# Layer 0's depthwise convolution in 64x64 tiles, with the work around it dealt out anew to ACT, POOL and DVE

## The chip, the cores and the metric

The kernel runs on one core of one Trainium2 chip. The metric is the device time in microseconds (us), the lower the better. The engines are TensorE (PE, with its weight loads shown as PEld), VectorE (DVE), ScalarE (ACT), GpSimd (POOL) and SyncE (SP, which here only issues DMAs). Each engine works through its own list of instructions in order; semaphores join the lists.

## The reference, cut to what matters

x is 8 samples of 256 positions by 256 features. Eight blocks follow each other, each added to x: cross-attention and a feed-forward part in each of four layers. The change lies in layer 0's feed-forward part, which for each sample is:

```
h = bit_linear(layernorm(x), w1)            # 256 -> 1024 features
h = silu(depthwise_conv1d(h, conv_w) + b)   # 3 taps over positions, each feature by itself
x = x + bit_linear(h, w2)                   # 1024 -> 256 features
bit_linear(x, w): per position, s = 127 / max|x|; round(x*s)/s, times w rounded to -1, 0, 1 (times mean|w|)
```

So each sample needs two maxima of absolute values per position: one over 256 features (in rows: positions on the partitions), one over 1024 hidden features (these lie on the partitions, 8 blocks of 128), and a rounding after each.

## The kernel before, in words

The stage is `ffn0`. Its lists are written out by hand: `ffn0_pe`, `ffn0_act`, `ffn0_dve` and `ffn0_pool`, each a loop over the samples i = 0 to 7; no planner orders them. In the round of sample i the stage works at once on the convolution of sample i, the first product of sample i+1 and the second product of sample i-1. Constants: B = 8 samples, S = 256 positions, T = 2 tiles of 128 positions, FC = 8 hidden blocks, PAIRS = 4 pairs of blocks.

One sample goes through these steps, with the lines of the profile. **Rows in:** DVE takes mean and variance (`ternary_stats`, L1290, L1293); POOL makes 1/sqrt (`ternary_rstd`, L198 and L201, a power); DVE normalizes (`quant_rows`, L1352), takes the largest absolute value (L1358), makes the scales in small instructions (L1363 to L1370), multiplies and rounds (L1372, L1374) and so releases `z_ready`. PE turns the rows (L1404, L1406), ACT copies them (L1393, L1394), PE makes the first product in pairs (L1417) and DVE multiplies each pair with the row of scales on its way out of PSUM (`first_kept`, L1381). **Convolution:** for each block PE adds up three products of a 128x128 diagonal matrix of taps with the block shifted by one position (`convolved`, L1642), all in f32. ACT adds the bias and takes the SiLU (`silus`, L1598) into one of two buffers `f_y`. **Second maximum:** DVE reduces four blocks at a time over the hidden blocks (`half_largest`, L1468), joins the halves (L1474), PE turns the result (`largest`, L1649), DVE reduces over the partitions and makes the scales (`scales`, L1479 to L1483), PE turns them back (`row2`, L1661), ACT copies them (L1588), POOL multiplies the SiLU's output with them in two halves (`scaled`, L1554), DVE rounds each half to bf16 (`rounded`, L1494), PE makes the second product (`second_made`, L1431), and DVE adds it to x (`second_added`, L1439).

Beside this PE makes the next attention's values and keys (`prepared`, L968, L1032) as filling, ACT keeps them (L800, L808, L809), and POOL clears a buffer in four pieces (`second_zeroed`, L1559). The last sample's second half is on DVE alone (`last_rounded`, L1504, L1505), its second product is made in the stage behind.

Rounding is an addition and a subtraction of 1.5 * 2^23: `v.tensor_scalar(f_aq[:, fs, :], f_y[i % 2][:, fs, :], ROUND, ROUND, ALU.add, ALU.subtract)`.

The rows of the weight w2 come by one DMA on SP's queue at 24.36 us and are there 7.4 us after; the first reader waits until 42 us or later.

## Time and profile before

| | |
|---|---|
| runs | 1155.62, 1160.81, 1163.85 us; median 1160.81 us |
| profiled execution | span 1158.0 us, the first to the last instruction; its own time is not given apart from the span |
| PE busy | 1103.8 us (95% of the span) |
| DVE busy | 772.5 us (67%) |
| POOL busy | 522.9 us (45%) |
| ACT busy | 430.0 us (37%) |
| mean granted TensorE clock | 0.989 of full speed |
| stage `ffn0` | about 138 to 285 us |

Busy time is an average over stages with different limits; the stage is read by itself in the rows below. Matmuls are pipelined, so a busy PE need not be at its peak.

### The profile page before, as it was taken

What the parts mean: (1) busy time and instruction counts of PE and PEld (TensorE: products, weight loads), DVE (VectorE), ACT (ScalarE), POOL (GpSimd) and SP (SyncE); (2) the same over time, 40 slices, a digit from 0 to 9 for tenths busy, and PEclk for the clock granted to TensorE, in tenths of its full rate; (3) what the DMA queues carried; (4) which work ended last, traced back from release to release, by engine and by line L of the source; (5) the groups of instructions that cost most, each with busy time, mean ns of one, the idle gap of its engine ahead of it and who ended that gap; (6) DMA issues with size and microseconds to landing.
All of it is one profiled execution on the core that took longest, in us unless ns stands there. A gap on an engine that the chain in (4) does not pass through costs nothing.

```text
span 1158.0 us, 21241 instructions
## 1 busy us (share of the span) xinstructions
PE 1103.8 (95%) x7601; PEld 919.3 (79%) x7601; DVE 772.5 (67%) x1711; ACT 430.0 (37%) x890; POOL 522.9 (45%) x505
## 2 busy tenths in 40 slices
PE   9999999999899999999989999999999999999997
PEld 5788888886778856898877999999998687875564
DVE  5899889997887645989962222222222899977784
ACT  2555533234555412121111222222222456654466
POOL 5655224356877121768866111100254757531343
PEclk9999999999999999999988999999999999999999
DMA  6999700000100020000135422311120200000001
GB/s 223 393 397 387 286 1 1 13 12 10 79 1 1 1 103 1 1 2 24 38 137 197 176 109 109 110 36 36 55 88 30 78 10 10 1 1 1 1 28 46
DMA packets 44182, 93.61 MB, mean 81 GB/s; under 512 B 3885, under 2 KB 17998, under 8 KB 41414
## 3 DMA queue, kind: packets, MB, share of 16 engines
q1 hardware_dynamic: 35702, 62.24, 14.9%
q0 software_dynamic: 7104, 29.14, 6.9%
q10 hardware_dynamic: 1296, 1.18, 0.3%
q8 instruction: 49, 0.80, 0.3%
q14 instruction: 31, 0.25, 0.1%
HBM read 39.02 MB, written 51.51 MB: 78 GB/s over the span
## 4 chain that ended last, share of the span: by engine, by line
PE 61%; DVE 21%; POOL 6%; issue 5%; ACT 4%; DMA 2%; POOLq 1%; PEldq 0%; another core or an unknown queue 0%; SPq 0%; DVEq 0%; PEld 0%; ACTq 0%
PE PS L2416 10%; PE PS L2426 10%; PE PS L1109 6%; PE PS L1925 4%; PE PS L2281 3%; PE PS L1122 3%; PE PS L1087 2%; PE PS L1077 2%; DVE scr L1468 2%; PE PS L2270 2%; PE PS L1642 2%; DVE scr L1494 2%; PE PS L1804 2%; POOL big L695 1%; PE PS L1035 1%
## 5 line engine op out<-in xcount | busy, mean ns | idle before, releaser
L2450 ACT ACTIVATE scr<-PS,W 128x128 f32<-128x128 f32 x148 | 53.6, 367 | 191.1 <-PE PS L2416 190.0
L2416 PEld LDWEIGHTS PS<-scr 128*128 128x128 f32 x992 | 116.4, 192 | 5.2 <-issue 2.0
L2416 PE MATMUL PS<-scr 128*128 128x128 f32 x992 | 118.6, 276 | 1.6 <-issue 1.6
L2426 PE MATMUL PS<-scr 128*128 128x256 f32 x496 | 112.2, 379 | 0.0
L2481 DVE TENSOR_SCALAR scr<-PS,W 128x128 f32<-128x128 f32 x148 | 51.2, 350 | 85.2 <-PE PS L2416 85.2
L727 POOL TENSOR_TENSOR scr<-scr,small 128x1232 f32<-128x1232 f32 x32 | 72.0, 2251 | 73.1 <-DVE small L478 72.8
L2426 PEld LDWEIGHTS PS<-scr 128*128 128x128 f32 x496 | 91.8, 190 | 11.2
L2487 DVE TENSOR_TENSOR scr<-PS,W 128x256 f32<-128x256 f32 x37 | 15.7, 425 | 127.1 <-PE PS L2426 122.3
L868 ACT ACTIVATE big<-PS 128x512 f32<-128x512 f32 x144 | 73.1, 523 | 69.1 <-PE PS L1087 67.7
L2527 POOL DMA_DIRECT2D expert_out<-scr x28 | 15.3, 547 | 160.5 <-DVE scr L2487 156.5
L1109 PEld LDWEIGHTS PS<-scr,big 128*128 128x128 f32 x640 | 81.0, 191 | 8.1 <-issue 5.1
L1642 PE MATMUL PS<-big,W 128*128 128x256 f32 x384 | 85.6, 379 | 0.0
L1087 PE MATMUL PS<-W,scr 128*128 128x128 f32 x480 | 76.3, 279 | 9.5 <-ACT big L846 3.0
L1109 PE MATMUL PS<-scr,big 128*128 128x34 f32 (+1 forms) x640 | 83.5, 271 | 1.0 <-ACT big L868 0.9
L1642 PEld LDWEIGHTS PS<-big,W 128*128 128x128 f32 x384 | 71.5, 189 | 9.6
L1087 PEld LDWEIGHTS PS<-W,scr 128*128 128x128 f32 x480 | 56.6, 150 | 20.3 <-ACT big L846 4.6
L1554 POOL TENSOR_TENSOR scr<-scr 128x1024 f32<-128x1024 f32 x14 | 32.9, 2373 | 68.0 <-ACT scr L1588 68.0
L2281 PE MATMUL PS<-W,scr 128*128 128x128 f32 x512 | 61.1, 278 | 2.5 <-DVE scr L2036 2.4
L2281 PEld LDWEIGHTS PS<-W,scr 128*128 128x128 f32 x512 | 58.5, 192 | 3.7 <-DVE scr L2036 3.5
L1804 PE MATMUL PS<-identb 128*128 128x512 bf16 x232 | 59.8, 400 | 0.3 <-ACT big L868 0.3
L863 ACT ACTIVATE scr<-scr 128x1232 f32<-128x1232 f32 x48 | 58.7, 1223 | 3.0 <-POOL scr L727 2.6
L1598 ACT ACTIVATE scr<-PS,W 128x256 f32<-128x256 f32 x64 | 26.9, 472 | 81.4 <-PE PS L1642 81.4
(418 smaller groups left out, 2496.4 us busy)
## 6 DMA issues: line engine op xcount, KB each, us to landing
expert_in<-zeros SPq DMA_DIRECT2D x1, 19712.0 KB, 60.5
expert_out<-zeros SPq DMA_DIRECT2D x1, 19712.0 KB, 113.2
scr<-ew_in POOLq DMA_DIRECT2D x12, 1024.0 KB, 6.6
scr<-expert_in SPq DMA_DIRECT2D x38, 128.0 KB
big<-ew_in POOLq DMA_DIRECT2D x4, 1024.0 KB, 8.9
expert_out<-scr POOLq DMA_DIRECT2D x28, 128.0 KB, 2.0
W<-pack SPq DMA_DIRECT2D x1, 2458.0 KB, 8.7
W<-pack SPq DMA_DIRECT2D x1, 2152.0 KB, 9.0
```

Of the source, the lines that this page charges most:

```text
L727: g.tensor_tensor(sc3, sc3, a_mx[u % 3].unsqueeze(2).broadcast_to([P, H, S2]), ALU.subtract).then_inc(s["sub_ready"], 1)
L863: a.activation(a_sc[lay][u % 3], a_sc[lay][u % 3], ACT.Exp, scale=scale).then_inc(s["p_ready"], 1)
L868: a.activation(a_PT[lay][u % 2][:, 4 * g:4 * g + n, :], bank(ring_bank(lay, "p", u, g), n * P).rearrange("p (c n) -> p c n", c=n), ACT.Cop ...
L1087: ins = pe.transpose(bank(b, P, k * P), a_sc[lay][u % 3][:, at:at + P], ident)
L1109: ins = pe.matmul(bank(6 + u % 2, n * (DH + 1), FIRST[c] * (DH + 1)), a_PT[lay][u % 2][:, c, :], a_VB[lay][:, c, 0:n, u // T, :], start=(c ...
L1642: ins = pe.matmul(bank(2 + p % 2, S, (f % 2) * S), f_taps[:, f, j, :], f_G[:, f, j:j + S], start=(j == 0), stop=(j == 2))
L1804: pe.matmul(bank(b, size, at), identb[:, :], identb[:, :].unsqueeze(1).broadcast_to([P, size // P, P]), start=True, stop=True)
L2281: ins = pe.matmul(bank(4, P, c * P), vp[:, t, c * P:(c + 1) * P], ident, start=(t == 0), stop=(t == B - 1))
L2416: ins = pe.matmul(bank(1 + f % 4, G), e_w1[slot][:, k, f * P:(f + 1) * P], e_xT[:, k, :], start=(k == 0), stop=(k == C - 1))
L2426: ins = pe.matmul(bank(5 + t, D), e_h[:, f, t * P:(t + 1) * P], e_w2[slot][:, f, :], start=(f == 0), stop=(f == FC - 1))
L2450: a.activation(e_h[:, f, :], bank(1 + f % 4, G), ACT.Relu, bias=moe_bias(e, f)).then_inc(s["h_act"], 1)
L2481: v.tensor_scalar(e_h[:, f, :], bank(1 + f % 4, G), moe_bias(e, f), 0.0, ALU.add, ALU.max).then_inc(s["h_dve"], 1)
```

## The change

**Convolution (PE).** A tap matrix is diagonal, so only its two 64x64 blocks on the diagonal hold anything. Each 128x128 product becomes two of 64x64; for a pair of blocks the four row and column quarters of the array are used: row half r, column half c. That takes 12 products for a pair in place of 6. The hidden features lie in another order afterwards, so w2's rows are loaded in that order by four DMAs of half the partitions each instead of one (SP's queue, ahead of the last part of the constants), and ACT makes the bias in that order by four small copies behind the attention before. Each pair now uses two PSUM banks.

**ACT** takes the normalized rows from DVE (`rows`) and makes |y| in two halves of 4x256 (`absolutes`). **DVE** takes the maximum of |y| by elementwise maxima, 512 wide twice, 512 and 256. **POOL** makes a shift beside the 1/sqrt and takes over both halves of the rounding, behind clearing and 1/sqrt. **Order:** `scales(i)` comes in round i, and no longer at the head of round i+1; DVE's `quantized(i+1)` therefore comes right behind the last `hidden` of the round before; the second product of sample i-2 is made in round i in place of that of i-1, and that of sample 6 after the last `largest`. Buffers for the factors of the second product become three. The stage `tail` reuses semaphores of this stage.

```diff
+        f_top = cut(4 * S).rearrange("p (n f s) -> p n f s", n=2, f=2)
         f_amax = cut(S)
+        f_abs = [t.rearrange("p (f s) -> p f s", f=PAIRS) for t in (cut(PAIRS * S), big[:, 3 * C * S * 2:3 * C * S * 2 + PAIRS * S])]
...
+        f_deq2 = [csmall(T) for _ in range(3)]
+        f_bias = csmall(FC)
...
+        HALF = P // 2
+        IN_FFN = 16 * (2 + 4)
+
+        def hidden_halves(t):
+
+            return t.rearrange("p (u r n) -> p u r n", u=PAIRS, r=2)
+
+        def hidden_rows_sp(sp):
+
+            new, old = hidden_halves(f_w2), hidden_halves(w2T_in)
+            for c in range(2):
+                for r in range(2):
+                    sp.dma_start(new[c * HALF:(c + 1) * HALF, :, r, :],
+                                 old[r * HALF:(r + 1) * HALF, :, c, :]).then_inc(in_ffn, 16)
+
+        def hidden_biases(a):
+
+            a.wait_ge(in_ffn, IN_FFN)
+            new, old = hidden_halves(f_bias), hidden_halves(w["conv_b"])
+            for c in range(2):
+                for r in range(2):
+                    a.activation(new[c * HALF:(c + 1) * HALF, :, r, :], old[r * HALF:(r + 1) * HALF, :, c, :],
+                                 ACT.Copy).then_inc(ffn0["w_ready"], 1)
...
+        ROW2 = [4] * (B - 1) + [0]
+        KV_BANK = [4] * (B - 1) + [6]
+        AMAX_BANK = 0
+
+        def conv_bank(i, p, r):
+
+            return (2, 3)[r] if p % 2 == 0 else (0, 1)[r] if (i, p) == (B - 1, PAIRS - 1) else (5, 6)[r]
...
-                quant_rows(v, ch, i)
+                v.wait_ge(s["rows_ready"], i)
...
-                v.wait_ge(s["silu_ready"], PAIRS * i + 2 * n + 2)
-                ch.inc(v.tensor_reduce(f_top[:, n, :], f_y[i % 2][:, n * PAIRS:(n + 1) * PAIRS, :].rearrange("p f s -> p s f"),
-                                       AX.X, ALU.max, apply_absolute_value=True))
+                v.wait_ge(s["abs_ready"], 2 * i + n + 1)
+                v.tensor_tensor(f_top[:, n, :, :], f_abs[n][:, 0:2, :], f_abs[n][:, 2:4, :], ALU.max).then_inc(s["abs_used"], 1)
 
             def largest(i):
 
-                ch.sync()
-                v.tensor_tensor(f_amax, f_top[:, 0, :], f_top[:, 1, :], ALU.max).then_inc(s["amax_ready"], 1)
+                v.wait_ge(s["abs_used"], 2 * i + 2)
+                ch.link(v.tensor_tensor(f_top[:, 0, :, :], f_top[:, 0, :, :], f_top[:, 1, :, :], ALU.max))
+                v.tensor_tensor(f_amax, f_top[:, 0, 0, :], f_top[:, 0, 1, :], ALU.max).then_inc(s["amax_ready"], 1)
...
-            def rounded(i):
-
-                if i:
-                    v.wait_ge(s["o_psum"], i)
-                for n in range(2):
-                    fs = slice(n * PAIRS, (n + 1) * PAIRS)
-                    v.wait_ge(s["scaled_ready"], 2 * i + n + 1)
-                    v.tensor_scalar(f_aq[:, fs, :], f_y[i % 2][:, fs, :], ROUND, ROUND, ALU.add,
-                                    ALU.subtract).then_inc(s["aq_ready"], 1)
...
             for i in range(B):
-                if i:
-                    scales(i - 1)
                 if i + 1 < B:
                     quantized(i + 1)
+                if i == B - 1:
+                    sample_stats(v, ch, 1, 1)
+                half_largest(i, 0)
                 if i + 2 < B:
                     ternary_stats(v, ch, i + 2)
+                elif i == B - 2:
+                    sample_stats(v, ch, 1, 0)
                 else:
-                    sample_stats(v, ch, 1, i + 2 - B)
-                half_largest(i, 0)
-                if i == B - 1:
                     sample_rows(v, 1, 1)
-                if i:
-                    rounded(i - 1)
-                if i == B - 1:
                     sample_stats(v, ch, 1, 2)
                     query_vars(v, ch, 0)
-                half_largest(i, 1)
-                largest(i)
                 if i + 1 < B:
                     hidden(i + 1, (0, 1))
-                if i:
-                    second_added(v, i - 1)
+                half_largest(i, 1)
                 if i + 1 < B:
-                    hidden(i + 1, (2, 3))
+                    hidden(i + 1, (2,))
+                largest(i)
+                scales(i)
+                if i >= 2:
+                    second_added(v, i - 2)
+                if i + 1 < B:
+                    hidden(i + 1, (3,))
                 if i >= 5:
                     key_vars(v, ch, i - 5)
                 if i == B - 2:
                     sample_rows(v, 1, 0)
-            scales(B - 1)
+            second_added(v, B - 2)
...
-            def scaled(i):
+            def scaled(i, n):
                 g.wait_ge(s["row2_ready"], i + 1)
-                for n in range(2):
-                    fs = slice(n * PAIRS, (n + 1) * PAIRS)
-                    y = f_y[i % 2][:, fs, :]
-                    g.tensor_tensor(y, y, f_row2.unsqueeze(1).broadcast_to([P, PAIRS, S]),
-                                    ALU.mult).then_inc(s["scaled_ready"], 1)
+                y = f_y[i % 2][:, n * PAIRS:(n + 1) * PAIRS, :]
+                g.tensor_tensor(y, y, f_row2.unsqueeze(1).broadcast_to([P, PAIRS, S]),
+                                ALU.mult).then_inc(s["scaled1_ready" if n else "scaled0_ready"], 1)
+
+            def rounded(i, n):
+                if i:
+                    g.wait_ge(s["o_psum"], i)
+                fs = slice(n * PAIRS, (n + 1) * PAIRS)
+                g.wait_ge(s["scaled1_ready" if n else "scaled0_ready"], i + 1)
+                g.tensor_scalar(f_aq[:, fs, :], f_y[i % 2][:, fs, :], ROUND, ROUND, ALU.add,
+                                ALU.subtract).then_inc(s["aq1_ready" if n else "aq0_ready"], 1)
...
             for i in range(B):
                 if i:
-                    scaled(i - 1)
-                if i + 2 < B:
-                    ternary_rstd(g, i + 2)
+                    scaled(i - 1, 1)
+                    scaled(i - 1, 0)
                 if i == 1:
                     g.wait_ge(at_["o_full"], NT)
                 if 1 <= i <= 4:
                     second_zeroed(i - 1)
+                if i + 2 < B:
+                    ternary_rstd(g, i + 2)
+                if i:
+                    rounded(i - 1, 0)
+                    rounded(i - 1, 1)
...
+            def rows(i):
+
+                a.wait_ge(rstd_ready, i + 1)
+                a.wait_ge(z_ready, T * i)
+                for t in range(T):
+                    ins = a.activation(f_z[:, t, :], X[:, T * i + t, :], ACT.Identity,
+                                       bias=f_shift[i % 2][:, t:t + 1], scale=f_rstd[i % 2][:, t:t + 1])
+                ins.then_inc(s["rows_ready"], 1)
+
+            def absolutes(i, n):
+
+                a.wait_ge(s["silu_ready"], PAIRS * i + 2 * n + 2)
+                if i:
+                    a.wait_ge(s["abs_used"], 2 * i + n - 1)
+                a.activation(f_abs[n], f_y[i % 2][:, n * PAIRS:(n + 1) * PAIRS, :], ACT.Abs).then_inc(s["abs_ready"], 1)
...
+            rows(1)
             for i in range(B):
                 silus(i, 0)
-                silus(i, 1)
                 if i:
                     row2(i - 1)
+                silus(i, 1)
+                absolutes(i, 0)
                 if i == B - 1:
                     extra_kept(a, 1, "z", 0)
                 silus(i, 2)
+                if i + 1 < B:
+                    normed(i + 1)
+                silus(i, 3)
+                absolutes(i, 1)
+                if i + 2 < B:
+                    rows(i + 2)
                 if i == B - 1:
                     extra_kept(a, 1, "q", 0)
-                silus(i, 3)
-                if i + 1 < B:
-                    normed(i + 1)
                 if i < 4:
-                    values_kept(a, 1, i, 5)
+                    values_kept(a, 1, i, KV_BANK[i])
                 else:
-                    rows_kept(a, i - 4, 5)
+                    rows_kept(a, i - 4, KV_BANK[i])
...
-                for f in (2 * p, 2 * p + 1):
-                    for j in range(3):
-                        ins = pe.matmul(bank(2 + p % 2, S, (f % 2) * S), f_taps[:, f, j, :], f_G[:, f, j:j + S],
-                                        start=(j == 0), stop=(j == 2))
+                for j in range(3):
+                    for r in range(2):
+                        rows = slice(r * HALF, (r + 1) * HALF)
+                        for c in range(2):
+                            f = 2 * p + c
+                            ins = pe.matmul(PS[c * HALF:(c + 1) * HALF, conv_bank(i, p, r), 0:S],
+                                            f_taps[rows, f, j, rows], f_G[rows, f, j:j + S],
+                                            start=(j == 0), stop=(j == 2))
...
+            pe.wait_ge(at_["y_done"], PTILE(0, NT - 2) + 1)
             for i in range(B):
                 convolved(i, 0)
                 convolved(i, 1)
                 if i:
                     row2(i - 1)
-                if i == B - 1:
-                    extra_made(pe, 1, "z", 0)
                 convolved(i, 2)
                 if i == B - 1:
                     pe.wait_ge(s["row2_ready"], i)
+                    extra_made(pe, 1, "z", 0)
+                convolved(i, 3)
+                if i == B - 1:
                     extra_made(pe, 1, "q", 0)
-                convolved(i, 3)
                 if i + 1 < B:
                     normed(i + 1)
+                if i >= 2:
+                    if i == 2:
+                        pe.wait_ge(s["w_ready"], C + 4 + 1)
+                    second_made(pe, i - 2)
+                for p in range(PAIRS - 1):
+                    if i + 1 < B:
+                        hidden(i + 1, p)
                 prepared(i)
                 if i + 1 < B:
-                    hidden(i + 1, 0)
-                    hidden(i + 1, 1)
-                if i:
-                    if i == 1:
-                        pe.wait_ge(s["w_ready"], 3)
-                    second_made(pe, i - 1)
+                    hidden(i + 1, PAIRS - 1)
                 if i == B - 1:
-                    clocked(pe, 6, 8)
+                    pe.wait_ge(s["silu_ready"], PAIRS * i + PAIRS - 1)
+                    clocked(pe, 2, 8)
                 largest(i)
-                if i + 1 < B:
-                    hidden(i + 1, 2)
-                    hidden(i + 1, 3)
+            second_made(pe, B - 2)
```

## Rows read from the trace of the kernel before

**Rows 1.** Stretches of the stage: us; each engine busy (instructions); clock, DMA, GB/s.

```profile
155.69:255.44 99.75, 99.56 (x591) 84.60 (x590) 96.23 (x188) 31.48 (x75) 45.68 (x30) 1.00 0.03 8
255.44:284.70 29.26, 27.80 (x166) 21.97 (x165) 23.45 (x50) 11.97 (x25) 16.45 (x9) 1.00 0.00 1
```
**Rows 2.** Order of time, 172 to 189 us: start, us, engine, line, operation, tiles, count.

```profile
172.19 5.35 PE L1642 MATMUL PS<-big,W 128*128 128x256 f32 x24
...
173.62 0.41 DVE L1479 TENSOR_REDUCE small<-PS 128x2 f32<-128x256 f32 x1
...
174.94 0.73 DVE L1352 TENSOR_SCALAR big<-X,W 128x256 f32<-128x256 f32 x2
...
175.71 0.69 DVE L1358 TENSOR_REDUCE small<-big 128x2 f32<-128x512 f32 x1
176.43 0.17 DVE L1363 TENSOR_SCALAR small<-small 128x2 f32<-128x2 f32 x1
...
178.09 0.43 DVE L1374 TENSOR_SCALAR W<-big 128x512 bf16<-128x512 f32 x1
...
178.77 4.68 POOL L1554 TENSOR_TENSOR scr<-scr 128x1024 f32<-128x1024 f32 x2 [9.40 <-ACT scr L1588]
...
181.24 3.35 DVE L1494 TENSOR_SCALAR scr<-scr 128x1024 bf16<-128x1024 f32 x2
...
182.78 0.27 PE L1404 MATMUL PS<-W 128*128 128x128 f32 x1
...
184.98 1.04 PE L1417 MATMUL PS<-big,W 128*128 128x256 bf16 x8
...
187.60 0.38 PE L1649 MATMUL PS<-W,scr 128*128 128x128 f32 x2
...
188.03 0.87 DVE L1439 SCALAR_TENSOR_TENSOR X<-PS,small,X 128x256 f32<-128x256 f32 x2
```
**Rows 3.** Groups by line, 110 to 290 us: shapes, count | busy us, mean ns | idle.

```profile
L1468 DVE TENSOR_REDUCE scr<-scr 128x256 f32<-128x1024 f32 x16 | 30.9, 1934 | 4.9 <-ACT scr L1598 4.9
L1598 ACT ACTIVATE scr<-PS,W 128x256 f32<-128x256 f32 x64 | 26.9, 472 | 81.4 <-PE PS L1642 81.4
L1381 DVE TENSOR_TENSOR big<-PS,W 128x512 f32<-128x512 f32 x32 | 20.6, 684 | 1.0 <-PE PS L1417 0.8
```
**Rows 4.** Order of time, from 126 us: the first sample's quantization.

```profile
126.37 2.25 POOL L727 TENSOR_TENSOR scr<-scr,small 128x1232 f32<-128x1232 f32 x1 [3.77 <-DVE small L478]
...
127.16 1.48 DVE L1363 TENSOR_SCALAR small<-small 128x2 f32<-128x2 f32 x1
```
**Rows 5.** Order of time, from 297.5 us: POOL and DVE in turn.

```profile
298.01 2.19 POOL L710 TENSOR_TENSOR X<-X,W 128x512 f32<-128x512 f32 x2
298.15 2.20 DVE L423 TENSOR_SCALAR big<-X,small 128x256 f32<-128x256 f32 x2 [0.67 <-POOL small L201]
```
**Rows 6.** Order of time, from 268 us: small powers on POOL.

```profile
270.89 0.69 POOL L201 TENSOR_TENSOR small<-small,neghalf 128x2 f32<-128x2 f32 x1
...
271.55 5.43 POOL L695 TENSOR_TENSOR big<-big,neghalf 128x32 f32<-128x32 f32 x1
...
275.69 0.17 DVE L1480 TENSOR_SCALAR small<-small 128x2 f32<-128x2 f32 x1
```
**Rows 7.** Order of time, 55 to 62 us: products in 32-row tiles.

```profile
58.38 0.81 PE L1077 MATMUL PS<-scr,big 32*128 32x154 f32 x16
...
59.12 1.09 PE L1109 MATMUL PS<-scr,big 128*128 128x34 f32 x8
```
**Rows 8.** ACT's groups by line over the whole span.

```profile
L863 ACT ACTIVATE scr<-scr 128x1232 f32<-128x1232 f32 x48 | 58.7, 1223 | 3.0 <-POOL scr L727 2.6 <-DVE scr L467 0.4
...
L876 ACT ACTIVATE scr<-X,small 128x256 f32<-128x256 f32 x16 | 8.7, 591 | 1.9 <-POOL small L209 1.9
```
**Rows 9.** POOL's writing without reading, 110 to 290 us.

```profile
L1559 POOL MEMSET scr<- 128x1224 f32 x2 | 2.2, 1120 | 0.0
```
**Rows 10.** Order of time, from 135 us: the table load ahead of the first SiLU.

```profile
139.97 1.28 ACT L1598 ACT_TABLE_LOAD   x1
```

91 lines of the change are left out of this document (49 added, 42 removed).

## The prediction

> **What bounds the kernel now.** I read the stretches first, since the change touches one stage. Between the convolutions of samples 1 and 7 there are six rounds in 99.75 us, 16.6 us each; PE is busy for 99.56 of them, but DVE for 96.23 too, ACT for 31 and POOL for 46 [rows 1]. So two engines are full at once, and relieving PE alone gives nothing. The order of time [rows 2] shows what fills them. PE: 24 of a round's 48 convolution instructions take 5.35 us with the last one's tail, so about 0.216 us each and 10.4 us a round; all else on PE is 6.2 us. DVE: two reductions of 1.93 us [rows 3], and the two roundings, 3.35 us together. That last number is the one to see: the first of them starts at 181.24, just behind the start of POOL's second multiplication (the two run from 178.77 for 4.68 us), and the pair takes 3.35 us where the instruction's own work is below 0.7 us each. DVE waited there for POOL.
>
> The same wait in its purest form: a DVE instruction on 2 elements, usually 0.17 us [rows 2], takes 1.48 us when it meets a POOL multiplication that ends at 128.62 [rows 4]. And where two DVE instructions meet two POOL ones, they alternate: each DVE one waits out one POOL one, and two of them take 2.20 us in place of the 0.73 us of two like them [rows 5, 2]. Reductions aren't held: L1468 begins beside POOL's first multiplication in most rounds and still takes 1.93 us on the mean [rows 3].
>
> **The change part by part**, T = 0 being the end of a round's `largest` on PE, everything for one round in steady state.
>
> *Convolution.* 96 instructions of 64x64 in place of 48. Rows of the trace with tiles: 16 instructions with 32 rows and 154 columns start at 58.38, and the next product can start at 59.12: 0.046 us each where 154/256 of 0.216 is 0.130 us, so 2.8 times as fast with the way in and out of the tiling, four side by side [rows 7]. I take four side by side: 96 x 0.216 / 4 = 5.2 us, plus 0.25 us for a change of tiling and back, twice (0.74 us less 4 x 0.130). Bounds: row halves alone side by side, 10.4 us; nothing side by side, 20.8 us. I stay with 5.2 because the row halves are shown and the column halves touch other outputs. No row has column tiles. The Trainium skill, TensorE: Matmul & The Clock Gate, Part 3, gives 2.38 times for three column tiles; by it 5.2 us would be an estimated 6.6 us, and my sum would rise by 1 us at most, since PE waits anyway. Saved on PE: 4.7 us a round.
>
> *DVE loses* the reductions (3.9), the roundings (3.4), L1352 (0.73) and gains 512-wide maxima (0.66 each by the pace of L1381's 0.68 [rows 3], three of them) and one of 256 (0.4): 2.4 us for the 0.4 of before. It falls from 16 to about 10.5 us. *ACT gains* two |y| of 1024: 1.05 us each (1.22 us for 1232 columns at 0.83 ns [rows 8]; bounds 0.9 to 1.2), and two normalizing tiles, 0.54 each [rows 8]; it stays under 9 us. *POOL gains* two roundings of 1024 and a longer 1/sqrt (1.5 us: 0.69 for the power [rows 6] and three small ones of about 0.27). POOL has no such rounding in the trace: the lower bound is a write alone, 1.12 us for 1224, so 0.94 for 1024 [rows 9]; the upper bound is its two-input product, 2.34 us [rows 2]. One input lies nearer to the write: 1.1 us. The Trainium skill, GPSIMD Engine Reference, section 3.1, has 1.03 cycles an element for short bodies; by it the estimate is 0.9 us and the sum 2.4 us less. POOL then works 4.7 + 2.2 + 1.5 + 1.1 = 9.5 us.
>
> By busy time nobody is above 11.5 us. But almost every DVE instruction that is left reads SBUF alone, and POOL is now at work for most of the round, so the held instructions decide. **The loop:**
> - to 3.7: PE makes two pairs (2.6), changes tiling (0.25), turns the scales (0.3), ACT copies them (0.4); POOL starts its two multiplications.
> - Meanwhile DVE: scales 1.3 (173.62 to 174.94) [rows 2], `second_added` 0.87, last `hidden` 0.64, the reduction L1358 0.70: at 3.8 it stands before L1363, just behind POOL.
> - L1363 waits until 6.1, L1364 for the second multiplication until 8.6. From there L1364 to L1374 take 1.8 us (176.6 to 178.4) [rows 2]: 10.4. Without waits it would be 5.9. PE, which needs this for its next turn, has been idle since 6.2.
> - PE's turn and ACT's two copies 1.7 (12.1), SiLU 0.84 (13.0; its last pair now stands behind these copies on ACT), |y| 1.05 (14.1).
> - POOL's 1/sqrt waits for DVE's statistics behind all this (12.0), so until 13.5, and then two roundings until 15.8. DVE's second half maximum waits for them: 16.5; `hidden` 0.64, two more maxima 1.05: 18.2; PE's turn: 18.5.
>
> So a round of 18.5 us instead of 16.6. Drawn through with the same durations, the first two of the six come to 17.0 and 17.6, mean about 17.8: 6 x 1.2 = +7.2. The first round (15.54 us) has no multiplication on POOL and comes to 13.1: -2.4. It starts later than it could: ACT now makes two tiles of rows (1.08) and four small bias copies ahead of the table load of 1.28 us [rows 10]. The last piece (29.26 us [rows 1]) gains in convolution, but the second product of sample 6 (1.9) and DVE's addition now lie between the last maximum and the last sample's rounding: +1.4. SP issues three DMAs more, about 1.4 us ahead of the last constants; the first reader comes over 10 us later, so nothing. The wait for `y_done` ahead of the first convolution asks for an addition two tiles back, nothing.
>
> Sum: 7.2 - 2.4 + 1.4 = +6.2; 1158.0 + 6.2 = 1164.2 for the profiled execution, which lies 2.8 below the median: **1167 us**.
>
> One rule speaks for still more waiting. The trace has small powers on POOL of 5.43 us, and beside one a two-number instruction of DVE takes its usual 0.17 us [rows 6], so I let only multiplications and roundings hold DVE. The Trainium skill, SBUF — State Buffer, "Who interferes with whom", says the shared ports are held for the whole instruction; by that rule the powers would add up to 1 us a round. The measurement decides.
>
> **Rivals.**
> - *Faster: the waits don't line up.* If DVE comes to L1363 some 2 us before POOL, or its row of seven instructions passes together once it has its turn, the round falls to what remains: 18.5 less 4.5 (quantization) and 1 (maxima) = 13.1 us by the same drawing without any hold, -3.5 x 6, and in all about -26: 1135 us. One wait only, not two, gives 1150. For it: DVE and POOL meet within 0.1 us in my drawing, so small shifts matter. Against it: moving the meeting by 1 us changes which instruction waits, not that two do, and the alternation in rows 5. Chance 0.30.
> - *Slower: POOL's rounding costs like its product.* 2.34 us in place of 1.1; both lie between the 1/sqrt and DVE's maximum, so 2.2 us a round, +14: 1181 us. It decides from about 1.6 us on, where the time passes the 1% mark. For it: POOL does two operations and a conversion. Chance 0.13.
> - *The tiles don't do what they say:* column halves one after the other. PE then has 10.4 + 6.2 + the changes; round 18.7 to 19 us, +13 on top of my sum: 1180 us; with nothing side by side 29 us a round, beyond 1240. Chance 0.10, the latter 0.02 of it.
> - PE idle for over 4 us in each round may cost granted clock, now 1.00 throughout the stage [rows 1]; PE has slack there, so I count at most 1 us a round, within the range.
>
> **How the numbers follow.** About 1%, 11.6 us, is what can be told from no change: faster is below 1149, slower above 1172. The forecast's own case has 0.44 and runs from 1159 to 1177; 0.36 of it is within 1% and 0.08 above. The faster rival puts 0.28 below and 0.02 within. The two slow rivals (0.23) give 0.20 above and 0.03 within; the remaining 0.03 is spread. So faster 0.29, same 0.42, slower 0.29. As both signs hold much, the range must take in the unhindered case and the dear rounding: 1134 to 1182, with 0.1 left out at either end.
>
> **What will show it.** Right: DVE's L1363 and L1364 successors lasting 1.5 to 2.4 us beside POOL's products in each round; a gap on PE of about 4 us ahead of the turn of the next sample's rows; 96 convolution instructions in about 5.5 us; rounds of 17 to 18.5 us; POOL's rounding at 1.0 to 1.3 us. Wrong: DVE's small instructions at 0.2 us there and rounds of 13 to 14 us, or a POOL rounding above 1.6 us, or convolution instructions at 0.1 us each and more.

## The result, and the profile after

The change made the kernel slower: 1193.95 us (median of 4 runs, 1189.18 to 1197.85) against 1159.93 us before (1155.62 to 1163.85), a ratio of 1.030 (95% interval 1.026 to 1.034). I had forecast 1167 us in a range of 1134 to 1182, so the time lies outside the range. The profiled execution spans 1189.3 us, the one before 1158.0: +31.3. One of the four executions of the kernel with two buffers below (1195.59 us) fell in a slower state that shows a lower granted clock, and its figures leave that one out.

All of it lies in this stage. The last second product (L1431 before, L1463 now) ends at 284.7 before and at 316.2 now, +31.5; what follows takes 873.3 and 873.1 us. The stretches answer to [rows 1]: from the second sample's convolution to the last sample's, and from there to the end of the last second product.

```profile
154.83:266.94 112.11, 83.48 (x861) 55.99 (x860) 91.44 (x166) 48.17 (x97) 80.80 (x48) 0.88 0.03 7
266.94:316.24 49.30, 30.08 (x229) 20.42 (x229) 29.18 (x51) 14.05 (x27) 31.39 (x15) 0.79 0.00 1
```

Six rounds went from 99.75 to 112.11 us and the last piece from 29.26 to 49.30. PE, nearly full before, is now busy for 83 of 112 us; DVE for 91. POOL went from 46 to 81, and the granted clock of TensorE from 1.00 to 0.88 and 0.79. No engine is full: each now waits for the others. The groups of 138 to 317 us show which instructions grew (shapes, count | busy us, mean ns | idle before, releaser):

```profile
L1591 POOL TENSOR_SCALAR scr<-scr 128x1024 bf16<-128x1024 f32 x14 | 51.5, 3698 | 14.9 <-PE PS L1463 14.9
L1711 PE MATMUL PS<-big,W 64*64 64x256 f32 x768 | 48.4, 398 | 5.9 <-ACT scr L1643 5.9
...
L1463 PE MATMUL PS<-big,scr 128*128 128x256 bf16 x128 | 21.6, 341 | 2.3 <-DVE X L1471 2.3
...
L1402 DVE TENSOR_SCALAR big<-big,small 128x256 f32<-128x256 f32 x14 | 16.7, 1232 | 0.0
...
L1436 PE MATMUL PS<-W 128*128 128x128 f32 x14 | 4.9, 366 | 17.9 <-DVE W L1404 17.8
```

The same group of the second product before, from 110 to 290 us:

```profile
L1431 PE MATMUL PS<-big,scr 128*128 128x256 bf16 x128 | 15.3, 273 | 0.0
```

The first row is the surprise: POOL's rounding of one half takes 3.70 us, 7.3 us for a sample. L1402 (the multiplication of the quantization, L1372 before) shows the hold that I had looked for, a DVE instruction that lasts until POOL's is through: it takes 0.61 us for two when nothing is in the way, and 1.23 us for one on the mean here. The last is what it costs PE: 17.8 us of waiting for the quantized rows of L1404. One round in order of time (start, us, engine, line, tiles, count [idle before, releaser]):

```profile
205.44 3.63 POOL L1591 TENSOR_SCALAR scr<-scr 128x1024 bf16<-128x1024 f32 x1
...
209.19 0.84 ACT L1643 ACTIVATE scr<-PS,small 128x256 f32<-128x256 f32 x2 [3.59 <-POOL scr L1591]
...
210.17 2.82 PE L1711 MATMUL PS<-big,W 64*64 64x256 f32 x48 [1.16 <-ACT scr L1643]
...
210.38 4.71 POOL L1583 TENSOR_TENSOR scr<-scr 128x1024 f32<-128x1024 f32 x2 [1.31 <-ACT scr L1630]
210.43 5.87 DVE L1402 TENSOR_SCALAR big<-big,small 128x256 f32<-128x256 f32 x2
...
216.40 0.43 DVE L1404 TENSOR_SCALAR W<-big 128x512 bf16<-128x512 f32 x1
...
216.89 0.33 PE L1436 MATMUL PS<-W 128*128 128x128 f32 x1 [3.89 <-DVE W L1404]
...
217.39 3.09 PE L1463 MATMUL PS<-big,scr 128*128 128x256 bf16 x16
...
220.57 3.63 POOL L1591 TENSOR_SCALAR scr<-scr 128x1024 bf16<-128x1024 f32 x1 [0.69 <-PE PS L1463]
```

It reads as a circle. The roundings end, ACT's first SiLU of the next sample has waited 3.59 us for them, the convolution waits for ACT, and the row of scales lets POOL multiply. DVE's two L1402 meet the two multiplications and take 5.87 us. PE idles 3.89 us, then runs the second product, which takes 3.09 us, part of it at the lower clock, against 1.91 before (L1431, 282.76 to 284.67); and the next rounding waits for that product, since it writes the buffer that it reads. The stretches during PE's wait and in the second product (the number after POOL's instructions is the clock):

```profile
212.00:216.00 4.00, 0.99 (x20) 0.47 (x12) 4.00 (x2) 0.85 (x3) 4.00 (x3) 1.00 0.00 0
218.50:220.50 2.00, 2.00 (x12) 1.38 (x11) 0.00 (x0) 1.97 (x4) 1.22 (x4) 0.50 0.19 50
```

PE is busy for 0.99 of 4 us, and then works at half clock, 1.2 GHz.

The last two samples lose most. POOL's queue carries the powers of attention 1 behind the roundings:

```profile
261.39 7.44 POOL L1591 TENSOR_SCALAR scr<-scr 128x1024 bf16<-128x1024 f32 x2 [6.62 <-PE PS L1463]
...
269.78 5.91 POOL L681 TENSOR_TENSOR small<-small,neghalf 77x16 f32<-77x16 f32 x2
...
272.94 5.06 DVE L423 TENSOR_SCALAR big<-X,small 128x256 f32<-128x256 f32 x2
...
275.51 4.70 POOL L1583 TENSOR_TENSOR scr<-scr 128x1024 f32<-128x1024 f32 x2
...
286.17 7.23 POOL L1591 TENSOR_SCALAR scr<-scr 128x1024 bf16<-128x1024 f32 x2 [5.97 <-PE PS L1463]
...
294.39 0.74 DVE L423 TENSOR_SCALAR big<-X,small 128x256 f32<-128x256 f32 x2 [13.63 <-POOL small L201]
...
298.69 0.69 PE L1719 MATMUL PS<-W,scr 128*128 128x128 f32 x2 [9.15 <-DVE scr L1515]
```

The multiplications of sample 6 start at 275.51, behind L681, though their row of scales was copied by 270.55; DVE's two L423 (0.74 us at 294.39) take 5.06 us at 272.94, as the first waits out a power, L681, and the second a multiplication, and PE waits 6.55 us for them; DVE then waits 13.63 us for a reciprocal root that stands behind the last pair of roundings, and the last maxima stand behind that on DVE, so PE waits 9.15 us for them.

### The profile page after: what moved, and what is told of

Read it like the earlier page. It is cut to its first block, busy times and chain, and to the rows that moved or that the text cites. A ratio compares the mean times of both kernels' runs of the same rounds, so it can differ in the third digit from the quotient of the medians.

```text
span 1189.3 us, 22100 instructions
## 1 busy us (share of the span) xinstructions
PE 1088.7 (92%) x7985; PEld 887.0 (75%) x7985; DVE 771.1 (65%) x1691; ACT 453.6 (38%) x924; POOL 573.1 (48%) x533
## 4 chain that ended last, share of the span: by engine, by line
PE 60%; DVE 18%; POOL 9%; issue 6%; ACT 4%; DMA 2%; POOLq 1%; PEldq 0%; DVEq 0%; SPq 0%; ACTq 0%; PEld 0%
PE PS L2484 10%; PE PS L2494 10%; PE PS L1109 6%; PE PS L1993 3%; PE PS L2349 3%; PE PS L1122 3%; PE PS L1087 2%; PE PS L1077 2%; PE PS L2338 2%; PE PS L1872 2%; POOL big L695 1%; PE PS L1035 1%; DMA expert_out<-scr 1%; DVE big L1402 1%; POOL scr L1591 1%
## 5 line engine op out<-in xcount | busy, mean ns | idle before, releaser
L1591 POOL TENSOR_SCALAR scr<-scr 128x1024 bf16<-128x1024 f32 x14 | 51.5, 3698 | 14.9 <-PE PS L1463 14.9
L695 POOL TENSOR_TENSOR big<-big,neghalf 128x32 f32<-128x32 f32 x8 | 45.0, 5620 | 24.0 <-DVE big L431 23.7
L1122 PE MATMUL PS<-W,big 128*128 128x256 f32 x192 | 53.6, 402 | 0.8 <-ACT big L889 0.7
L1711 PE MATMUL PS<-big,W 64*64 64x256 f32 x768 | 48.4, 398 | 5.9 <-ACT scr L1643 5.9
```

The lines of the kernel that those rows point to most:

```text
L695: g.tensor_tensor(a_qr[j % 2], a_qvar[j % 2], neghalf[:, 0:T * H], ALU.pow).then_inc(s["qr_ready"], 1)
L1122: ins = pe.matmul(bank(6 + u % 2, D, D), a_OT[lay][:, c, :], wo[:, c, :], start=(c == 0), stop=(c == C - 1))
L1591: g.tensor_scalar(f_aq[:, fs, :], f_y[i % 2][:, fs, :], ROUND, ROUND, ALU.add, ALU.subtract).then_inc(s["aq1_ready" if n else "aq0_ready"], 1)
```

## The experiments

Three properties of the changed kernel turned out to matter: who rounds, when POOL's multiplications start, and the convolution's tiles. The times, with the distances between the starts of successive pairs of multiplications read from each trace; and how long the six rounds and the last piece of the stage are, bounded as the two stretches above:

| kernel | us | ratio to before, 95% | rounds between multiplications, us | six rounds | last piece |
|---|---|---|---|---|---|
| before | 1157 to 1160 | | 16.5 x5, 17.3 | 99.8 | 29.3 |
| changed: tiles, rounding on POOL | 1193.95 | 1.030 (1.026 to 1.034) | 17.9 16.7 17.3 19.4 20.3 25.4 | 112.1 | 49.3 |
| changed, rounding on DVE | 1180.11 | 1.019 (1.015 to 1.023) | 18.4 19.5 20.3 20.6 19.6 20.5 | 118.9 | 36.2 |
| changed, late multiplications | 1171.14 | 1.011 (1.008 to 1.015) | 16.3 17.3 16.5 17.3 16.7 20.1 | 99.4 | 44.6 |
| changed, both | 1154.90 | 0.997 (0.995 to 0.999) | 15.1 16.1 15.4 15.9 15.5 12.8 | 92.1 | 36.3 |
| changed, whole tiles | 1179.46 | 1.019 (1.015 to 1.022) | 16.8 17.4 17.4 17.4 17.4 21.1 | 103.7 | 45.0 |
| whole tiles, rounding on DVE | 1174.74 | 1.015 (1.011 to 1.020) | 18.0 18.6 18.6 18.6 18.6 18.6 | 110.8 | 33.6 |
| whole tiles, both | 1176.26 | 1.015 (1.012 to 1.018) | 18.0 18.6 18.6 18.6 19.2 17.9 | 110.9 | 34.9 |

"Late multiplications" and "both" are explained below. The kernel before has medians of 1157.3 to 1159.9 us in the four sets of runs, and what follows the stage, the same code in all, takes 869.2 to 876.5 us in the profiled executions; so a difference of 2 or 3 us between two rows is not settled, and the last two columns say more about the stage than the totals.

**Rounding back on DVE.**

```diff
-                if i:
-                    rounded(i - 1, 0)        # POOL
-                    rounded(i - 1, 1)
...
                 if i + 1 < B:
                     hidden(i + 1, (0, 1))
+                if i:
+                    rounded(i - 1)           # DVE, both halves
                 half_largest(i, 1)
```

> The changed kernel with one part undone: both halves of the rounding are back on DVE (after the first two pairs of the next sample's hidden values), POOL keeps the two multiplications. Theory A (POOL's rounding is the loss): in the changed kernel the pair of roundings takes 7.23 to 7.5 us on POOL against the 2.2 us I summed, it lies between the second product of the sample before and the first silu of the next sample, and in the last two samples the powers of attention 1 stand behind it on POOL. Then this kernel loses all of it: rounds of 16 to 17 us, 1135 to 1165 us. Theory B (the loss is DVE held by POOL's multiplications, 4.7 us a round, which stay): 1180 to 1195 us. Theory C (the loss is TensorE's granted clock at its lower level in the stage, for another reason than idle time caused by the rounding): 1175 to 1195 us with a mean clock still near 0.966.

1180.11 us (1178.86 to 1182.29), clock 0.973. Theory A alone is refuted: 14 us came back, not 30 to 60. And the table shows where: the last piece is 13.1 us shorter, while the six rounds are 6.8 us longer, as DVE now has the roundings and PE waits 25.0 us for L1404 in place of 17.8. So in the six rounds the dear rounding was no loss against this kernel; its price lies in the last two samples. Theory B's range (1180 to 1195 us) and theory C's (1175 to 1195) both hold the time; C is taken up with the idle work below. The trace shows B in its barest form. In four of the six rounds POOL's pair now starts among DVE's two-element steps:

```profile
194.78 4.66 POOL L1595 TENSOR_TENSOR scr<-scr 128x1024 f32<-128x1024 f32 x2 [10.30 <-ACT scr L1631]
194.95 2.22 DVE L1394 TENSOR_SCALAR small<-small 128x2 f32<-128x2 f32 x1
...
197.09 0.15 DVE L1395 RECIPROCAL small<-small 128x2 f32<-128x2 f32 x1
197.27 2.91 DVE L1396 TENSOR_SCALAR small<-small 128x2 f32<-128x2 f32 x1
199.38 0.79 POOL L1600 MEMSET scr<- 128x816 f32 x1
...
201.14 0.43 DVE L1404 TENSOR_SCALAR W<-big 128x512 bf16<-128x512 f32 x1
...
201.62 0.47 PE L1436 MATMUL PS<-W 128*128 128x128 f32 x1 [4.52 <-DVE W L1404]
```

Steps of 0.23 and 0.17 us take 2.22 and 2.91; the one between them, a reciprocal, is not held. L1396 outlasts the second multiplication: it ends with POOL's clearing of a buffer (L1600) behind it. It takes 3.25 us in the next round, where the clearing takes 1.12 us, and 2.20 in the one after, which has none. So the clearing holds DVE as well, and that adds 0.7 and 1.05 us. PE waits 4.52 us.

**A second buffer for the rounded values.**

```diff
-                if i:
-                    g.wait_ge(s["o_psum"], i)
+                if i >= 2:
+                    g.wait_ge(s["o_psum"], i - 1)
...
-                g.tensor_scalar(f_aq[:, fs, :], ...
+                g.tensor_scalar(f_aq[i % 2][:, fs, :], ...
```

> The changed kernel with a second buffer for the rounded hidden values, so that POOL's rounding no longer waits until the second product of the sample before has read the one buffer. In the changed kernel that wait ends 1.5 to 6.6 us after POOL is free in rounds 4 to 7. Theory A1 (it is the place of the rounding behind the second product, behind DVE's held quantization, that makes the rounds 19.4, 20.3 and 25.4 us long): these go back to about 17 us, 1168 to 1180 us. Theory A2 (the length of the rounding by itself fills POOL's queue, in the last two samples above all, where the powers of attention 1 stand behind it): 1183 to 1196 us.

1178.77 us (1177.34 to 1183.93, 3 runs): by the time alone, within A1's range. But rounds 4 and 5 still take 18.95 and 20.30 us, so the wait for the second product was not what made them long: A1 is wrong there. Only the last went from 25.4 to 20.1 us, as the roundings, and the powers behind them, start earlier. The six rounds take 110.9 us in place of 112.1, and the last piece 38.8 in place of 49.3: there the wait for the buffer cost some 10 us.

**The rounding alone moved to POOL, in the kernel before.**

```diff
                     second_zeroed(i - 1)
+                if i:
+                    rounded(i - 1)           # POOL; DVE's call is taken out
```

> The kernel before with one part of the change alone: both halves of the rounding on POOL, behind the row statistics' power; all else as before. There the second product of the same round waits for the rounding. Theory A (3.6 to 3.7 us a half wherever it stands): the pair ends about 6 us later than DVE's did, rounds of 20 to 23 us in place of 16.5, 1185 to 1210 us. Rival (the 3.7 us come from what runs beside it in the changed kernel, the |y| of ACT and the halving maxima of DVE, and a half takes at most 2.34 us here): 1160 to 1175 us.

1210.79 us (1209.25 to 1211.49), just above theory A's range, and its rounds of 23.6 to 25.9 us lie above the 20 to 23 expected.

```profile
L1552 POOL TENSOR_SCALAR scr<-scr 128x1024 bf16<-128x1024 f32 x14 | 50.7, 3639 | 0.0
...
L1431 PE MATMUL PS<-big,scr 128*128 128x256 bf16 x128 | 26.2, 377 | 35.3 <-POOL scr L1552 35.3
```

The price is 3.64 us here too, without ACT's |y| or DVE's halving beside it. The changed kernel, with all its other parts, is 17 us faster than this one; which of them hides that much was not taken apart.

**Rounding on DVE, whole convolution tiles.**

```diff
-                for j in range(3):
-                    for r in range(2):
-                        ... PS[c * HALF:(c + 1) * HALF, conv_bank(i, p, r), 0:S]
+                for f in (2 * p, 2 * p + 1):
+                    for j in range(3):
+                        ins = pe.matmul(bank(conv_bank(i, p, f % 2), S), f_taps[:, f, j, :], ...
```

> As the first kernel of this set (rounding on DVE), with the convolution back in whole 128x128 tiles, 24 matmuls of 256 columns a round in place of 96 in 64x64 tiles, in the same banks and order. By the rows the tiles save 10.7 - 5.6 = 5 us of TensorE a round. If TensorE bounds a round of the first kernel, this one is slower by up to 8 x 5 = 40 us; if DVE and the chain around it do, by 0 to 10 us. I expect 5 to 20 us more than the first kernel.

(The trace has two records for each matmul of f32 numbers. So 96 records are 48 matmuls, in 64x64 tiles, and the whole tiles are 48 records or 24 matmuls. The expectation for late multiplications with whole tiles, below, takes 0.446 us for a record; it is the time of a matmul, 10.7 us a round.) 1174.74 us (1173.60 to 1178.24): 5 us *faster* where I expected 5 to 20 slower, though PE has 5 us more to do in each round. The order of time tells why: the convolution ends later, so the multiplications begin when the quantization is through.

```profile
198.24 0.43 DVE L1404 TENSOR_SCALAR W<-big 128x512 bf16<-128x512 f32 x1
...
198.91 5.12 POOL L1595 TENSOR_TENSOR scr<-scr 128x1024 f32<-128x1024 f32 x2 [11.04 <-ACT scr L1631]
```

The 64x64 tiles gave their 5 us, and with them brought POOL's start onto the quantization: that was the reading here, and it pointed to the next runs.

**Late multiplications**, with the rounding on DVE:

```diff
                 if i:
+                    if i + 1 < B:
+                        g.wait_ge(z_ready, T * (i + 2))   # next sample's rows are quantized
                     scaled(i - 1, 1)
                     scaled(i - 1, 0)
```

> As the kernel with the rounding on DVE (1180 us), and POOL starts its two multiplications only when DVE has quantized the next sample's rows. In that kernel's trace the multiplications (4.66 us a pair) start between two of DVE's small steps of the quantization: two instructions that take 0.23 and 0.17 us alone take 2.22 and 2.9 to 3.25 us, TensorE waits 4.5 to 4.9 us a round for the quantized rows, and its granted clock in the stage is 0.91. Theory B (DVE held by the multiplications, at this place, is the rest of the loss): the wait of TensorE goes, rounds of 15 to 17 us, clock 0.98 or more in the stage, 1145 to 1165 us. Rival (the chain from |y| through the maxima to the row of scales is the bound, or the multiplications hold other instructions for as long): 1172 to 1185 us.

1154.90 us (1153.60 to 1157.20, 10 runs), 25 us less for one wait *added*. The small steps and PE's turn:

```profile
202.69 0.23 DVE L1394 TENSOR_SCALAR small<-small 128x2 f32<-128x2 f32 x1
...
203.02 0.17 DVE L1396 TENSOR_SCALAR small<-small 128x2 f32<-128x2 f32 x1
...
204.15 0.43 DVE L1404 TENSOR_SCALAR W<-big 128x512 bf16<-128x512 f32 x1
204.66 5.14 POOL L1595 TENSOR_TENSOR scr<-scr 128x1024 f32<-128x1024 f32 x2 [6.67 <-DVE W L1404]
...
206.45 0.33 PE L1436 MATMUL PS<-W 128*128 128x128 f32 x1
```

0.23 and 0.17 us again, and PE finds the rows ready. POOL waits 6.67 us. ACT waits for POOL behind it (for the shift, L209, 21.1 us in the stage), but it has room; of PE's and DVE's waits in the stage only one, of 0.9 us, is put down to POOL. The time is as theory B has it; the clock came back only in part, from 0.87 in the stage to 0.94, where B had 0.98.

**The same with the rounding on POOL** (the diff above on the changed kernel).

> The changed kernel (rounding on POOL) with the multiplications behind the quantization, as in the kernel before this one. Theory: hold and rounding each cost a part by themselves. The hold goes, but POOL's chain of multiplications 4.7, power 1.4, roundings 7.3 and ACT's wait for them stay: 1170 to 1185 us. Rival 1 (the hold was the whole cause and the rounding only made it longer): under 1165 us. Rival 2 (POOL is late anyway and the later start adds to it): 1195 to 1215 us.

1171.14 us (1169.66 to 1171.91): as the theory has it. The hold is worth 22.8 us here and 25.2 with the rounding on DVE; the rounding's place on POOL costs 13.8 with the hold and 16.2 without. One by one, from 1154.9, they cost 16.2 and 25.2, together 39.1: nearly their sum. Without the hold the rounding on POOL costs 7.2 us in the six rounds (99.4 against 92.1) and 8.3 in the last piece.

**The changed kernel with whole tiles.**

> The changed kernel (rounding on POOL) with the convolution in whole 128x128 tiles, 24 matmuls a round for 96. By the rows TensorE has 5 us a round more to do. If the 64x64 tiles are a gain by themselves: 1210 to 1235 us. With the rounding on DVE the whole tiles were 5 us faster (1174.7 against 1180.1), as the multiplications then start after the quantization and hold none of it; if that is the rule here too, 1185 to 1200 us.

1179.46 us (1178.09 to 1180.64), 14.5 us less than with the 64x64 tiles and 5 us below what I expected. On POOL the rounding costs only 5 us here (1174.74 with it on DVE): 7.1 us saved in the six rounds and 11.4 lost in the last piece. Why it saves here is not shown.

**Late multiplications, rounding on DVE, whole tiles.**

> The kernel with the rounding on DVE and late multiplications (1154.9 us) with the convolution in whole 128x128 tiles, 48 records of 0.446 us a round for 96 that take 5.6 us. With the whole tiles and without the late start it was 1174.7 us, and there the multiplications held none of the quantization, so the late start should change little: 1170 to 1177 us. Then the 64x64 tiles are worth 15 to 22 us here, where in the changed kernel they cost 14. Rival (the tiles never mattered): 1153 to 1160 us.

1176.26 us (1175.58 to 1176.92), as with the early start (1174.74): multiplications that miss the quantization cost nothing, early or late. So, with the rounding on DVE, the tiles are worth 21 us when nothing is held (1176.3 to 1154.9), and cost 5 to 14 when their early end makes POOL meet the quantization.

**Prices by themselves.** A kernel of its own with POOL, DVE and PE on fixed tiles; it leaves out the whole computation.

> Prices by themselves; the kernel computes nothing of the reference and writes x out. On POOL alone, 128x1024 f32 in, three of each: two-operation tensor-scalar to bf16 and to f32, one operation to f32 and to bf16, the product with a broadcast row to f32 and to bf16. Theory A: the two-operation form costs 3.6 to 3.7 us to bf16, alone as in the kernel, and the product 2.34. If the second operation is what costs, the one-operation forms take 1.8 to 2.4 us; if the bf16 output is, the f32 forms take under 2.4 us. Then DVE's tensor-scalar, small tensor-scalar, tensor-tensor and reduction beside eight products and beside eight roundings of POOL: held up to 2.3 us each beside the products, and at their own durations beside the roundings. On TensorE 60 whole f32 matmuls, 640 in 64x64 tiles and 60 whole, without a gap: if the tiles themselves lower the granted clock, it falls in the middle part, else it stays at 1.0.

```profile
L148 POOL TENSOR_SCALAR F<-IN 128x1024 f32<-128x1024 f32 x3 | 10.9, 3628 | 0.2
...
L200 POOL TENSOR_SCALAR F<-IN 128x1024 f32<-128x1024 f32 x3 | 8.3, 2770 | 0.2
L202 POOL TENSOR_SCALAR H<-IN 128x1024 bf16<-128x1024 f32 x3 | 8.3, 2770 | 0.2
L206 POOL TENSOR_TENSOR H<-IN,ROW 128x1024 bf16<-128x1024 f32 x3 | 7.1, 2365 | 0.2
```

L148 is the two-operation form, 3.63 us to f32 (the three to bf16, at the start, took 11.05 us together); L200 and L202 have one operation, to f32 and bf16; L206 is the product. So the output's type costs nothing, the second operation 0.86 us, and one operation with one input is dearer than the product of two. DVE beside POOL's products, and then beside its roundings:

```profile
59.95 7.78 POOL L151 TENSOR_TENSOR F<-IN,ROW 128x1024 f32<-128x1024 f32 x3
60.05 2.28 DVE L175 TENSOR_SCALAR VO<-SM 128x2 f32<-128x2 f32 x1
62.37 0.69 DVE L176 TENSOR_TENSOR VO<-V 128x512 f32<-128x512 f32 x1
63.10 0.69 DVE L177 TENSOR_REDUCE SM<-V 128x2 f32<-128x512 f32 x1
...
92.56 0.29 DVE L174 TENSOR_SCALAR VO<-V 128x256 f32<-128x256 f32 x1
92.89 0.88 DVE L175 TENSOR_SCALAR VO<-SM 128x2 f32<-128x2 f32 x1
```

A tensor-scalar of two elements takes 2.28 us beside a product (0.17 us alone, in the same trace) and at most 0.96 beside a rounding, one of 256 columns at most 1.12 there (0.29 alone); the reduction is never held. The tensor-tensor begins between two products and takes its 0.69, and three products take 7.78 us in place of 7.24 alone: there POOL waited for DVE. PE's f32 matmuls ran without a gap, whole ones, 640 in 64x64 tiles, whole ones again:

```profile
32.00:100.00 68.00, 68.00 (x1268) 47.93 (x1260) 40.45 (x49) 58.76 (x25) 1.00 0.01 2
```

The granted clock stays at 1.00 (2.4 GHz) in the tiles, so they don't lower it by themselves. 640 of them took 69.30 us, 0.108 us each: four in 0.433 us, the time of one whole matmul (the last 60 whole ones in 26.17 us, 0.436). Four lie side by side.

**Idle work on PE in the changed kernel.**

```diff
+                if 2 <= i < B - 1:
+                    if i >= 3:
+                        pe.wait_ge(s["o_kept"], i - 2)
+                    clocked(pe, 7, 16)
                 if i + 1 < B:
                     normed(i + 1)
...
-                if i == B - 1:
-                    pe.wait_ge(s["silu_ready"], PAIRS * i + PAIRS - 1)
-                    clocked(pe, 2, 8)
+                pe.wait_ge(s["silu_ready"], PAIRS * i + PAIRS - 1)
+                clocked(pe, 2, 8 if i == B - 1 else 5)
                 largest(i)
```

> The changed kernel with idle work on TensorE in its two long waits: 16 matmuls of 512 columns on a unit matrix before the next sample's rows are turned (rounds 2 to 6, where it waits 3.9 to 5 us for DVE's held quantization), and 5 before the maxima are turned. Nothing else is changed. Theory C (the granted clock, at its lower level in some 51 us of the stage, makes the second product 3.1 to 3.7 us long in place of 1.96 and so a real part of the loss): clock back to 0.98 or more, 1176 to 1187 us. Rival (the clock falls only because TensorE waits, and what it does slower lies beside other waits): 1190 to 1197 us at the better clock.

1183.16 us (1180.11 to 1184.52), clock 0.980: 10.8 us less for work that computes nothing, as theory C has it. In the profiled executions 7.0 us of it lie in the stage, 2.5 in the six rounds and 3.2 in the last piece; the rest lies behind it, in code that is the same.

```profile
L1463 PE MATMUL PS<-big,scr 128*128 128x256 bf16 x128 | 17.0, 291 | 2.3 <-DVE X L1471 2.3
```

The second product's matmuls fall from 341 to 291 ns. So the fall of the clock, which followed PE's waits, was a real part of the loss, but by the stage some 7 us and not 11. It overlaps with the other two, which cause those waits. In this trace no multiplication runs beside DVE's L423, only the powers L681:

```profile
266.32 5.79 POOL L681 TENSOR_TENSOR small<-small,neghalf 77x16 f32<-77x16 f32 x2
...
266.86 4.85 DVE L423 TENSOR_SCALAR big<-X,small 128x256 f32<-128x256 f32 x2
```

They take 4.85 us in place of 0.74: each waits out one power.

**Rounding later, on DVE.** The late multiplications, with the roundings behind `largest(i)`.

```diff
-                if i:
-                    rounded(i - 1)
                 half_largest(i, 1)
                 if i + 1 < B:
                     hidden(i + 1, (2,))
                 largest(i)
+                if i:
+                    rounded(i - 1)
```

> The kernel with the rounding on DVE and late multiplications (1154.9 us), with the rounding moved behind the largest magnitude, where DVE waits for TensorE anyway. In its trace the rounding takes 1.3 to 2.6 us ahead of the maxima, and TensorE waits 1.3 to 2.6 us a round for them (8.5 us in five rounds). If that wait is on the path, 7 x 1.3 to 2 us less: 1143 to 1149 us. Rival: the rounding now delays the row of scales, and with it nothing but the multiplications, or the first silu of the next sample waits for it: 1150 to 1157 us.

1148.32 us (1147.49 to 1149.89, 6 runs), 0.991 of before (0.989 to 0.993): the fastest, and faster than both kernels. Rounds of 12.4 to 14.9 us.

```profile
206.99 0.42 DVE L1515 TENSOR_TENSOR scr<-scr 128x256 f32<-128x256 f32 x1
...
207.33 1.29 DVE L1535 TENSOR_SCALAR scr<-scr 128x1024 bf16<-128x1024 f32 x2
207.47 0.44 PE L1722 MATMUL PS<-W,scr 128*128 128x128 f32 x2 [0.86 <-DVE scr L1515]
```

The roundings now run while PE turns the maxima and convolves; PE's wait for L1515 falls from 8.5 to 3.7 us in 176 to 260 us. The time is the one expected.

**The same with 5 idle matmuls before the maxima are turned.**

> As the kernel with the later rounding, with 5 idle matmuls before the maxima are turned (about 1.1 us of TensorE). If the clock at its lower level still lengthens the convolution there (2.82 to 4.51 us once in the trace of the kernel without it), up to 5 us less than without the fillers; if the idle matmuls come to lie on the path, up to 4 us more. I expect 1 to 3 us less.

1152.78 us (1150.93 to 1154.46): 4.5 us *more*, a miss. Up to the last second product the profiled execution is only 1.1 us longer; another 5.0 us come after the stage, in code that is the same. Whether an event of the stage does that or chance isn't settled. What can be said is that idle work was no gain here, where PE no longer waits long.

## Why the prediction was wrong, by its steps

- **POOL's rounding, 1.1 us: the first step that failed.** It measures 3.70 us. Not only the value: I had taken the two-input product (2.34) as the upper bound for an instruction with one input. The prices show the opposite: 2.77 us for one operation and 3.63 for two, against 2.37 for the product. The Trainium skill, GPSIMD Engine Reference, section 3.1, has 1.03 cycles an element, an estimate of 0.9 us by it; the measurement says three to four times that. The rival "costs like its product" had the right sign, but its price was too low (it gave 1181) and its place wrong: beside a rounding DVE's maxima get at most 0.7 us longer (L1515 1.14 for 0.42). Undone alone, the rounding on POOL is worth 13.8 to 16.2 us in time, as DVE then has the work; what it would be at 1.1 us on POOL no run shows.
- **The last piece, +1.4 us: the second step that failed.** It measures +20.0 (29.26 to 49.30 us). I drew only DVE's and PE's chains there. POOL's queue, with 7.3 us of rounding ahead of the powers of attention 1, was not followed to its end: L423's 13.63 us of waiting is the price. With the rounding on DVE the last piece falls to 36.2 us. So this is where the dear rounding costs.
- **That the sum comes near with the right price is luck.** With 3.70 in place of 1.10, twice in each of six rounds, it reads 1167 + 31 = 1198, and 1194 was measured. But it puts 38 us into the six rounds, where 12.4 were measured, and 1.4 into the last piece, where it was 20.0.
- **The hold of DVE: right in mechanism, and roughly in size.** DVE's tensor-scalar instructions wait out POOL's products, by 22.2 us in the six rounds of the trace, 3.7 a round where I drew 4.5, and PE idles for 3.8 to 4.3 us before its turn in four rounds, where I drew about 4. But L1363 and L1364, now L1393 and L1394, which I had named, are both held in only one round (1.79 and 2.26 us), and L1393 alone in another; in the other four POOL starts 0.9 to 1.4 us after L1393 and meets L1402 or L1404 (5.87 us for two L1402). I gave the hold 32 us against the unhindered case, with the rival at 1135; the late multiplications measure 22.8 to 25.2. I had let roundings hold DVE in full as well: beside them a tensor-scalar gets at most 0.8 us longer. I had left out the clearing, which does hold.
- **The unhindered round: 13.1 us drawn, 12.8 to 16.1 measured** with the rounding on DVE, 12.4 to 14.9 with it moved later. The best of these kernels took 1148 us, 13 above the rival's 1135.
- **Two sums don't come out as written.** Rounds of 17.0, 17.6 and four times 18.5 have a mean of 18.1, not 17.8, so the six rounds add 8.9 and not 7.2 us, and the forecast by its own terms is 1169. The unhindered case by its own terms is 21.0 + 2.4 - 1.4 = 22 us below before, not 26: 1139.
- **Convolution in four tiles at once: right.** 48 records of a half round take 2.82 us, 5.6 a round, where I had 5.2 plus 0.25 a change. The rival of tiles that lie one after the other is refuted.
- **ACT: right.** |y| 1.06 us (1.05), rows 0.54 each (1.08 a pair).
- **First round right:** 13.1 drawn, 13.17 from 141.66 to 154.83. It begins 1.5 us later than before; with the rounding on DVE, and the same code up to there, it begins at 140.01, so that is chance. **The six rounds: +7.2 forecast, +12.4 measured.**
- **The clock: at most 1 us a round forecast.** Idle work brought back 7.0 us in the stage of the profiled execution, 2.5 of it in the six rounds: the size was right. "PE has slack there" was wrong, as the second product stands on the chain after each wait, and the next rounding waits for it.
- **Powers, put at nothing: wrong in the last piece.** L666 takes 1.78 us beside one (0.18 alone) and L423 5.06, half of it behind a power; the kernel with idle work shows two held by powers alone. It isn't so each time: in the changed kernel with whole tiles two L423 take 0.74 us just as such a power starts (263.68). No run was made for it. The Trainium skill, SBUF — State Buffer, "Who interferes with whom", has the rule that whoever issues first has the shared pair for the whole instruction, and a tensor-reduce doesn't contend. The prices agree for products against tensor-scalar (2.28 us) and reductions (0.69), and, where DVE came first, for the product that waited; the held L423 agree too, the free ones don't; beside roundings the hold ends long before the instruction's 3.63 us do.

## What to carry to other kernels

Before work is moved to an engine that has no such instruction in the trace, take its price from a small run, and bound it from above generously: fewer inputs is no bound. When a change speeds up what stands ahead of a shared resource, ask what it will now collide with: here 5 us a round of faster convolution cost 5 to 14 us in all, until one added wait moved POOL's multiplications behind the quantization; then, with the rounding on DVE, it was worth 21. And follow every queue to which work is added to the end of the stage, where the next stage's first steps stand behind it.

## What the runs showed of the hardware

- POOL, 128x1024 f32: tensor-scalar 2.77 us with one operation, 3.63 with two, to bf16 or f32 alike; product with a broadcast row 2.37.
- Beside POOL's product a DVE tensor-scalar of 2 elements lasts up to 2.29 us (alone 0.17) and a reciprocal 0.15; beside POOL's two-operation tensor-scalar it lasts at most 0.96. POOL's clearing holds it too: 3.25 us with a clearing of 1.12 us behind the product, 2.20 without. A power of 2.9 us on POOL can hold a tensor-scalar of 256 columns (2.50 us, 0.37 alone).
- f32 matmuls in 64x64 tiles, two row halves and two column halves with outputs in two banks: four in 0.433 us, as one whole, at a granted clock of 1.00 throughout.
- In the changed kernel each of PE's four waits of 3.8 to 4.3 us is followed by the clock's lower level (0.50 of full, 1.2 GHz, in 165 to 168, 218.5 to 220.5, 236.5 to 239 and 257 to 260 us); 16 idle matmuls in each long wait brought the stretch from 180 to 260 us from 0.84 to 0.93 back to 1.00.
